# Four attention layers over graphs: layer 0's receiver factors are spread by transfers through memory and one transpose instead of sixteen

## What is computed

```python
h = jnp.maximum(_layernorm(x), 0.0)
x = x + L0(h, adj)   # 4 heads of 64 features
x = x + L1(h', adj)  # mlp, attention without a mask, mlp, masked attention
x = x + L2(h'', adj) # one head of 256, mask or diagonal
x = x + L3(h''', adj)
# inside layer 0, for each batch and head:
Wh = h @ W                                   # 512 nodes x 64
e  = leaky_relu(s_src[i] + s_dst[j], 0.2)    # 512 x 512
alpha = softmax_j(where(adj != 0, e, -inf))
out = elu(alpha @ Wh)
```

## Time and profile before

| | |
|---|---|
| median of 3 runs | 2927.38 us (2925.52 to 2928.27) |
| the profiled execution | 2929.61 us, of which the span of its trace is 2927.8 us |
| mean granted TensorE clock | 0.993 of full speed |
| TensorE matmuls busy | 98% of the span |
| VectorE, ScalarE, GpSimd busy | 84%, 79%, 7% |
| DMA | 42.06 MB, mean 14 GB/s |

### The profile page before, as it was taken

One profiled execution on the slowest core, in us unless ns is written; L12 is line 12 of the kernel. 1 busy time (PEld: TensorE's weight loads), 2 busy tenths in 40 slices (PEclk: granted clock), 3 DMA queues, 4 the chain that ended last, 5 costly groups with the idle time before them and its releaser, 6 DMA issues.

```text
span 2927.8 us, 66974 instructions
## 1 busy us (share of the span) xinstructions
PE 2867.1 (98%) x25624; PEld 2639.1 (90%) x25624; DVE 2450.5 (84%) x7049; ACT 2306.8 (79%) x6303; POOL 208.9 (7%) x410
## 2 busy tenths in 40 slices
PE   8999999999999999999999999999999999999997
PEld 7899999999999999999999999999999998999986
DVE  6788888888888888888888888888888888888866
ACT  6678778777788787788787787777787877887776
POOL 2000000000000000000000000000000000000000
PEclk8999999999999999999999999999999999999999
DMA  2000000000000000000000000000000000000000
GB/s 80 1 9 16 16 16 16 16 1 16 16 16 16 9 9 16 16 16 16 2 16 16 16 16 16 2 16 16 16 16 9 9 16 16 16 16 2 2 1 30
DMA packets 16367, 42.06 MB, mean 14 GB/s; under 512 B 5296, under 2 KB 6832, under 8 KB 16048
## 3 DMA queue, kind: packets, MB, share of 16 engines
q1 hardware_dynamic: 16048, 37.77, 3.7%
HBM read 20.99 MB, written 16.78 MB: 13 GB/s over the span
## 4 chain that ended last, share of the span: by engine, by line
PE 85%; ACT 9%; DVE 5%; issue 1%; SPq 0%; POOL 0%; DMA 0%
PE bank L515 45%; PE bank L584 23%; PE bank L620 7%; PE bank L536 4%; PE bank L572 3%; ACT junk L1022 3%; ACT junk L1031 2%; PE bank L672 1%; DVE O L916 1%; ACT Z L1175 1%; PE bank L560 1%; PE bank L698 1%; ACT Z L1068 1%; DVE oTlo L920 1%; ACT hT1hi L1177 0%
## 5 line engine op out<-in xcount | busy, mean ns | idle before, releaser
L584 PE MATMUL bank<-hw,R 128*128 128x257 f32 x3072 | 708.2, 381 | 1.7 <-ACT hw L1083 1.0
L584 PEld LDWEIGHTS bank<-hw,R 128*128 128x128 f32 x3072 | 566.5, 191 | 75.7 <-issue 3.6
L793 DVE SCALAR_TENSOR_TENSOR R<-bank,E,mask_ne 128x512 f32<-128x512 f32 x640 | 449.5, 743 | 3.2 <-PE bank L572 0.8
L1248 POOL TENSOR_TENSOR rs<-ve,mhalf 128x4 f32<-128x4 f32 x128 | 140.7, 1099 | 2661.2 <-DVE ve L745 1655.8
L1045 ACT ACTIVATE Z<-x,nm,rs 128x256 f32<-128x256 f32 x512 | 276.5, 594 | 53.0 <-DVE x L1010 32.1
L515 PE MATMUL bank<-wfc_hi,oThi 128*128 128x256 f32 (+1 forms) x1024 | 303.0, 296 | 0.0
L515 PE MATMUL bank<-wfc_hi,oTlo 128*128 128x256 f32 (+1 forms) x1024 | 289.6, 283 | 0.0
L515 PE MATMUL bank<-wfc_lo,oThi 128*128 128x256 f32 (+1 forms) x1024 | 289.5, 283 | 0.0
L620 PE MATMUL bank<-hw,R 128*64 128x65 f32 x8192 | 269.1, 224 | 0.3 <-DVE R L793 0.3
L620 PEld LDWEIGHTS bank<-hw,R 128*64 128x64 f32 x8192 | 251.1, 138 | 20.1 <-issue 9.9
L1068 ACT COPY Z<-bank 128x258 f32<-128x258 f32 (+1 forms) x512 | 180.8, 371 | 39.7 <-PE bank L515 39.3
(11 more groups left out here) (262 smaller groups left out, 8355.4 us busy)
## 6 DMA issues: line engine op xcount, KB each, us to landing
x<-in_x_dram SPq DMA_DIRECT2D x32, 512.0 KB, 3.4
out_dram<-x SPq DMA_DIRECT2D x32, 512.0 KB, 2.6
R<-in_adj_dram SPq DMA_DIRECT2D x2, 512.0 KB, 6.1
Z<-in_L_gnn_mlp_w_dram SPq DMA_DIRECT2D x2, 512.0 KB, 5.4
O<-in_L_gnn_W_fc_dram SPq DMA_DIRECT2D x1, 1024.0 KB, 7.0
R<-in_L_gnn_W_dram SPq DMA_DIRECT2D x1, 256.0 KB, 3.7
R<-in_L_gnn_W_hand_dram SPq DMA_DIRECT2D x1, 256.0 KB, 6.7
rowt<-in_L_gnn_W_dram SPq DMA_DIRECT2D x1, 256.0 KB, 4.7
```

The source lines that it names most:

```text
L584: ins = e.matmul(bk[:, 0:257], P[:, j, i * 128:(i + 1) * 128], hw[:, j, 0:257], start=(j == 0), stop=(j == NBLK - 1))
L793: e.scalar_tensor_tensor(P[:, t, :], bank_of(b, "row", p)[:, :], m["E"][:, 1, h, j:j + 1], mask[:, j, :], ALU.max, ALU.mult).then_inc(up(" ...
L1248: e.tensor_tensor(m["rs"][:, :], m["ve"][:, :], mhalf[:, :], ALU.pow).then_inc(up("rs", b))
```

## The change

Layer 0's receiver factors of all four heads are turned by one transpose (`rows0`: 128 x 16 becomes 16 x 128), copied by ScalarE into the first 16 partitions of `Sb`, written by SyncE to a small buffer in device memory (`rowd`, 8 KB), and read back by two transfers that repeat it on all 128 partitions, 512 KB each, into the two parts of `hT` of the lane, which are free between the projection of layer 0 and the transposes of layer 1: heads 0 and 1 in the high part, heads 2 and 3 in the low part. `weigh` reads them there instead of in PSUM. Layer 0 then uses one bank for rows instead of four. The rows of the other attentions stay as they were, with new numbers. Several semaphores are joined (`hA`, `hB`, `Phi` to `fhi`; `hAlo`, `hBlo`, `Plo` to `flo`). The filling matmuls of the first batch (`warm`) read weights instead of `hT`. All tables of `TURNS` are new; one line of them is shown.

```diff
@@ SHARED, ONCE, USES @@
-    "h": (5, 4), "raw": (5, 4), "sc": (5, 5), "TM": (5,), "E": (5, 3), "row": (8,),
+    "h": (5, 4), "raw": (5, 4), "sc": (5, 5), "TM": (5,), "E": (5, 3), "row": (5,),
-    + [("TM0", 0, "sc", (0, 1)), ("row", 0, "P", (0, 3))]
-    + [u for h in range(4) for u in (
-        ([("row", h + 1, "P", (h + 1, 3))] if h < 3 else []) + [("att0", h, "y0", (h,))])]
+    + [("TM0", 0, "sc", (0, 1)), ("row", 0, "rT", (0,))]
+    + [("att0", h, "y0", (h,)) for h in range(4)]
@@ TURNS @@
     "pool": (
-        ("wwwwwwww0wwwwwwwww10w0w20"),
+        ("wwwwwwwwwwwwww0w1ww0ww020"),
...
     "sp": (
-        ("0"),
-        ("32"),
-        ("2165544313200"),
+        ("00112020"),
+        ("2002"),
+        ("33554221413030112020"),
     ),
@@ build @@
+        rowd = nc.dram_tensor("rowd", [LANES, 2048], F32)
+        s_rowd = new_sem("rowd")
+        s_rows = [new_sem(f"rows_{p}") for p in PARTS2]
@@ tensor_batch @@
+            def rows0():
+                w.wait_ge(*freed(b, "row", 0))
+                bk = bank_of(b, "row", 0)
+                warm(bk, 14)
+                w.wait_ge(*at("E", b, 0, 0))
+                e.transpose(bk[0:16, 0:128], m["E"][:, 0, :, :].rearrange("p h n -> p (h n)"),
+                            ident[:, :]).then_inc(up("row", b))
+                yield
...
-            yield from row(0, 0, 0)
+            yield from rows0()
             for h in range(4):
-                if h < 3:
-                    yield from row(h + 1, 0, h + 1)
@@ vector_batch, weigh @@
-                w.wait_ge(*at("row", b, p))
+                if l == 0:
+                    w.wait_ge(s_rows[h // 2], 16 * (b + 1))
+                    row = f32(hT[s][PARTS2[h // 2]])[:, h % 2, :]
+                else:
+                    w.wait_ge(*at("row", b, p - 3))
+                    row = bank_of(b, "row", p - 3)[:, :]
...
-                    e.scalar_tensor_tensor(P[:, t, :], bank_of(b, "row", p)[:, :], m["E"][:, 1, h, j:j + 1],
+                    e.scalar_tensor_tensor(P[:, t, :], row, m["E"][:, 1, h, j:j + 1],
                                            mask[:, j, :], ALU.max, ALU.mult).then_inc(up("P", b))
@@ scalar_batch @@
             yield from exps(0, 4, 0.2, hv[:, :, :, 64].rearrange("p b h -> p h b"))
+            w.wait_ge(*at("row", b, 0))
+            e.copy(m["Sb"][0:16, 0:128], bank_of(b, "row", 0)[0:16, 0:128]).then_inc(up("rT", b))
+            yield
@@ sync_batch @@
-            n = b + LANES
+            s, n = b % LANES, b + LANES
+            w.wait_ge(*at("rT", b, 0))
+            if b:
+                w.wait_ge(s_rowd, 16 * b)
+            e.dma_start(rowd[s, :].rearrange("(k n) -> k n", n=128), sm[s]["Sb"][0:16, 0:128]).then_inc(s_rowd, 16)
+            yield
+            w.wait_ge(s_rowd, 16 * (b + 1))
+            for k, p in enumerate(PARTS2):
+                if b:
+                    w.wait_ge(s_rows[k], 16 * b)
+                e.dma_start(f32(hT[s][p]).rearrange("p k n -> p (k n)"),
+                            rowd[s, k * 1024:(k + 1) * 1024].partition_broadcast(128)).then_inc(s_rows[k], 16)
+            yield
```

More of the change, by code:

```diff
@@ L54 @@
     + [("r3", i, "r3c", (i,)) for i in range(2)]
-    + [("h2", i, "raw", (2, i)) for i in range(4)] + [("TM2", 0, "sc", (2, 1)), ("row", 5, "P", (5, 3))]
+    + [("h2", i, "raw", (2, i)) for i in range(4)] + [("TM2", 0, "sc", (2, 1)), ("row", 2, "P", (5, 3))]
     + [("att0b", i, "yh", (i,)) for i in range(4)]
     + [("hT2", k, "hTlo", (2, k)) for k in range(2)] + [("h3", i, "raw", (3, i)) for i in range(4)]
-    + [("TM3", 0, "sc", (3, 1)), ("row", 6, "P", (6, 3))] + [("att1b", i, "e2", (i, 1)) for i in range(4)]
+    + [("TM3", 0, "sc", (3, 1)), ("row", 3, "P", (6, 3))] + [("att1b", i, "e2", (i, 1)) for i in range(4)]
     + [("hT3", k, "hTlo", (3, k)) for k in range(2)] + [("S", 1, "Sb", (1,))]
     + [("h4", i, "raw", (4, i)) for i in range(4)]
-    + [("TM4", 0, "sc", (4, 1)), ("row", 7, "P", (7, 3))] + [("att2b", i, "y3", (i,)) for i in range(4)]
+    + [("TM4", 0, "sc", (4, 1)), ("row", 4, "P", (7, 3))] + [("att2b", i, "y3", (i,)) for i in range(4)]
 )
@@ L525, in warm @@
                     for _ in range(n):
-                        e.matmul(bk[:, :], W0["hi"][:, 0, 0:128], hT[s]["hi"][:, 0, :], start=True, stop=True)
+                        e.matmul(bk[:, :], W0["hi"][:, 0, 0:128], W0["hi"].rearrange("p k n -> p (k n)")[:, 0:512], start=True, stop=True)
             m, hw, hv, P, hn = sm[s], hws[s], hvs[s], R[s], hns[s]
@@ L644, in tensor_batch @@
                 if n == 1:
-                    yield from row(4, 1, 0)
+                    yield from row(1, 1)
                 w.wait_ge(*freed(b, "hs2", n))
@@ L704, in tensor_batch @@
             yield from top(2, 1)
-            yield from row(5, 2, 0)
+            yield from row(2, 2)
             yield from attend(0, 2, 5)
@@ L713, in tensor_batch @@
             yield from top(3, 1)
-            yield from row(6, 3, 0)
+            yield from row(3, 3)
             yield from attend(1, 3, 6)
@@ L723, in tensor_batch @@
             yield from top(4, 1)
-            yield from row(7, 4, 0)
+            yield from row(4, 4)
             yield from attend(2, 4, 7)
@@ L809, in split_sums, with low_part @@
                 yield
-            def low_part(kind, name):
-                H = HA if kind == "hA" else HB[s]
+            def low_part(half, name):
+                H = (HA, HB[s])[half]
                 for n in range(NBLK):
-                    w.wait_ge(*at(kind, b, n))
+                    w.wait_ge(*at("fhi", b, half, n))
                     e.tensor_tensor(H["lo"][:, n, 0:F], bank_of(b, name, n)[:, 0:F], f32(H["hi"][:, n, 0:F]),
-                                    ALU.subtract).then_inc(up(kind + "lo", b))
+                                    ALU.subtract).then_inc(up("flo", b))
                     yield
@@ L873, in vector_batch @@
                 yield
-            yield from low_part("hA", "h1")
+            yield from low_part(0, "h1")
             yield from scores(1, 1)
-            yield from low_part("hB", "hs2")
+            yield from low_part(1, "hs2")
             w.wait_ge(*at("E", b, 1, 1))
@@ L1124, in scalar_batch @@
                 e.copy(raw[s][:, n, 256:258], bank_of(b, "h1", n)[:, 256:258]).then_inc(up("raw", b))
-                e.copy(HA["hi"][:, n, 0:F], bank_of(b, "h1", n)[:, 0:F]).then_inc(up("hA", b))
+                e.copy(HA["hi"][:, n, 0:F], bank_of(b, "h1", n)[:, 0:F]).then_inc(up("fhi", b))
                 yield
@@ L1132, in scalar_batch @@
                 w.wait_ge(s_wT, 7)
-            w.wait_ge(*at("row", b, 4))
-            e.copy(rowt[s][:, 0:512], bank_of(b, "row", 4)[:, :]).then_inc(up("rowc", b))
+            w.wait_ge(*at("row", b, 1))
+            e.copy(rowt[s][:, 0:512], bank_of(b, "row", 1)[:, :]).then_inc(up("rowc", b))
             yield
@@ L1137, in scalar_batch @@
                 w.wait_ge(*at("hs2", b, n))
-                e.copy(HB[s]["hi"][:, n, :], bank_of(b, "hs2", n)[:, 0:F]).then_inc(up("hB", b))
+                e.copy(HB[s]["hi"][:, n, :], bank_of(b, "hs2", n)[:, 0:F]).then_inc(up("fhi", b))
                 yield
@@ L1141, in scalar_batch @@
                 w.wait_ge(*at("P", b, 4, j))
-                e.copy(oT["hi"][:, j, :], R[s][:, j, :]).then_inc(up("Phi", b))
+                e.copy(oT["hi"][:, j, :], R[s][:, j, :]).then_inc(up("fhi", b))
                 yield
```

101 lines of the change are left out of this document (49 added, 52 removed).

## The result

The change takes **2940.89 us** (median of 4 runs, 2938.59 to 2942.64) against 2926.45 of the kernel before (4 runs, 2924.35 to 2928.27): a ratio of 1.0049 with a 95% interval of 1.0032 to 1.0067. It is slower by 14 us where 40 us less were forecast. The profiled execution took 2938.59 us, at a span of 2936.6.

A forecast was written before the change was run, and what follows sets the result against it. TensorE was taken to bound the kernel, 88.3 us busy in each 89.0 us period. Profiled 2929.6 - 46.4 (TensorE work) + 3 (waits behind weighs) + 3 (start) = 2889.2 us, median 2887; range 2870 to 2912.

The forecast's parts named there:

- a saving on TensorE counts in full as long as nothing else becomes late: Steady period: TensorE's work plus a little waiting sets it; 1.45 us a batch saved, 46.4 us in 32.
- with the row in SBUF I keep that: VectorE's weighs in layer 0: each still costs 0.66 us step by step when the row moves from PSUM.
- The removed work: TensorE in layer 0: four rows of transposes go, 1.76 us a batch, against one new transpose at 0.11.
- The finer cut: TensorE's stream: the new order changes line slightly more often, charged 0.2 us a batch.
- The transfers: SyncE's write and reads of layer 0's rows: 6.0 us, at most 10.7; no cost in the cycle, 3.0 us cover.
- the caution taken from the load of 0.2 KB: SyncE's 8 KB write, taken at 2.6 us: loads of 0.2 KB take 3.7, so smallness need not help.
- Head 0's 0.2 us of room: TensorE at L629 behind head 0's weighs: 0.2 us to spare, some batches wait, 0.1 us a batch, 3 us charged.
- The start: Batch 0's first weighs: nothing covers the 6.0 us of transfers there; 3 us charged, between 0 and 8.
- The two rivals that cost time: VectorE's first weigh waiting for late rows, 2941 us, chance 0.08; too little room at head 0, 2913 us, chance 0.12.
- the rival of late rows: Rows land after VectorE's first weigh is due, 1.7 us late at the upper end: 2941 us, slower; chance 0.08.
- The tight order: Rows on time, but little room at head 0 and like places gives waits of 0.9 us a batch: 2913; chance 0.12.
- a period that stays at 89 though TensorE's busy time fell: Steady cycle: a sign that the forecast is wrong; the forecast expected a period near 87.6 us, TensorE about 86.9 busy.

The follow-up runs named there:

- a_free3: The change with ScalarE's normalise of layer 3 reading ve and sx, so it waits for VectorE and not GpSimd's rs and nm: 2915.74 us, 0.9957 of the kernel before.
- a repair: The change with GpSimd making nm<-sx while it waits for VectorE's ve, leaving two of three operations behind ve: 2919.88 us, 0.9975 of the kernel before.

## Why the prediction was wrong

Forecast for the profiled execution 2889.2 us, measured 2938.6: 49 us apart. Of these 31 lie in the 25 periods between the ends of batches 0 and 25 (1.35 us each was to be saved, 0.12 was), 5 in the first batch (3 charged, 8 lost), and 13 behind batch 25, where 9 us of the other seven batches were to be saved and 4 were lost.

- **The failed step is "a saving on TensorE counts in full as long as nothing else becomes late".** It was stated and then checked for VectorE's weighs, for the transfers and for the waits behind them, but not for GpSimd: what the moved operand costs there was put at nothing, without a reason. The price of the operand ("with the row in SBUF I keep that") was taken for VectorE alone, and there it was right: a weigh takes 744 ns from SBUF and 743 from PSUM. What it did was to lengthen a neighbour's three small operations from 1.6 to 2.8 us, and ScalarE's normalise and TensorE's transposes stand behind these with 0.2 us of cover. That took back 0.94 us a batch, 25 us by `a_free3`, 21.5 of which a repair brought back. It is about half of the 49 us: freed of it (`a_free3`, 2915.7) the change is 10.5 us faster than the kernel before on the same chip (2926.3), and still above the range of 2870 to 2912.
- The Trainium skill ("SBUF — State Buffer", Who interferes with whom) has a rule for this: a VectorE instruction with two SBUF inputs contends with a GpSimd instruction that reads SBUF, and one with at most one SBUF input, outside its two-port modes, does not. The trace agrees with both halves (1.81 against 1.04 us for rs). The rule speaks against this change, and the prediction passed over it. It quoted another rule of the Trainium skill in its place ("VectorE: DVE Perf Modes", The TRN2 errata: by its figures, as an estimate, a weigh from SBUF is 65 ns cheaper), and that one no run here shows: 744 against 743 ns.
- **The removed work was sized right**: 1.65 us a batch net of the new transpose, measured 1.74. **The finer cut was too cheap**, the second term that failed: I took 0.2 us a batch, and the groups other than the layers' transposes took 0.71 more (layer 0's projection 0.60, L595 0.33, the rest -0.22), 16 us in 32 batches above the forecast. Of the 0.60, 0.36 is the wait for the second half of hT0lo, which no step had named; whether the other 0.35 comes from cuts was not tested.
- **The transfers were right**: 6.0 us of way forecast, 1.3 + 4.1 = 5.4 measured (4.9 for the second read); cost in the cycle nil, as forecast. The rows of heads 0 and 1 landed 3.2 us ahead of the first weigh in the median batch of the cycle, where 3.0 were forecast. The smallness of the write did help, against the caution taken from the load of 0.2 KB. The first read took 0.7 us more than the load of x before (3.4), the second, issued right behind it, 1.5 more; how much of this the 128 repetitions cost and how much the pair was not tested.
- **Head 0's 0.2 us of room held.** No wait at L629 was named, so the 3 us charged were not needed.
- **The start was right in kind, too small in size, and for the wrong reason**: 3 us charged for uncovered transfers, 8 measured, and they are there without transfers.
- The two rivals that cost time named lateness at L807 and at L629. The mechanism that decided was neither of them. That the rival of late rows came to 2941 us, the time measured, is chance: no row was late in the cycle. The tight order is nearest in kind, a new order with little room, but the place was another. What would make the prediction wrong was put well in one line, a period that stays at 89 though TensorE's busy time fell: 88.74.

## What to carry to other kernels

When an operand moves between PSUM and SBUF, price it on the engine that reads it and then on the one beside it: GpSimd's small operations next to VectorE instructions with two SBUF tensors were 1.7 to 2.8 times as long here. An engine at 7% of the span can set the period; what counts is the time from its input to its consumer, and work that needs no late input belongs ahead of the wait. A visible wait is worth its size only if the producer can come earlier: ask what fills the time ahead of it before moving a turn.
